# A two-layer graph network on one core: a tile in every 64 fetched by SyncE, 30 edge groups stored as cell matrices in pass 1, blocks normalized two at a time, and a second pass by a table of counts

## The chip, the cores and the metric

The program runs on one core of a Trainium2 chip. Its time is the device time of one execution in microseconds (us). The kernel before took 1641.12 us (median of 3 runs, 1638.93 to 1643.31).

## The reference

6250 nodes with 96 features and 100000 edges, sorted by destination. Exact GELU, no approximations:

```python
# layer 0, over edges (src -> dst)
e = concat(x[src], edge_attr)                     # 100000 x 128
msg  = gelu(e @ mW1 + mb1) @ mW2 + mb2
gate = sigmoid(gelu(e @ gW1 + gb1) @ gW2 + gb2)
agg  = segment_sum(msg * gate, dst)
h    = x + gelu(concat(x, agg) @ uW1 + ub1) @ uW2 + ub2
x    = layernorm(x + layernorm(h) * ln_g + ln_b)
# layer 1, GCN
deg  = segment_sum(edge_weight, dst) + 1;  dinv = rsqrt(deg)
g    = segment_sum((x @ W)[src] * dinv[src] * w * dinv[dst], dst) + self loop
x    = layernorm(x + g + b)
```

## The kernel before

The edges are cut into 98 groups of 8 tiles of 128 edges; the nodes into 49 blocks of 128. Each pass treats the groups in order.

**Pass 1.** For each group GpSimd gathers the 8 tiles of source rows from HBM by 8 indirect DMAs (`gathers`, L430) into one of 8 slots of `rows`; a slot comes free when TensorE has transposed the group that lay in it. In `step1` TensorE turns the rows (L520, into the PSUM pair `ps_xt`), multiplies them by both first-layer weights in two halves (L543, L546, into the pair `ps_hid`), and sums messages into a window of nodes by a matrix of ones and zeros (`window1`, L493, `ps_win`). ScalarE copies the turned rows (L769), takes the GELU (L784) and the gate's tanh (L803, `squash`); VectorE makes the 0/1 matrix (L1034), reduces the gate's logit (L1123, L1126), applies the gate (`gate1`, L1099 to L1102) and adds the window to `acc1` (L1051). Every second group one block of nodes is finished: `agg`, `upd_in`, `upd_out` on TensorE (L593 to L611), `upd_gelu` on ScalarE (L814), `block1a` on VectorE, which normalizes twice with an inverse root by Newton steps (`rsqrt`, L1081 to L1090).

**Cell matrices.** For some groups of pass 2 the sum over sources isn't gathered but computed as a product of all node features with a matrix of "cells" (source node by destination column). 24 of these matrices are made in pass 1, two tiles per step from group 2 on: `pair_hot` on VectorE (L1133, L1137), `pair_cells` on TensorE (L571, one tile through `ps_xt` at the step's start, one through `ps_hid` at its end), `pair_copy` on ScalarE (L824) into one of two buffers, and a store of both tiles by SyncE (L406) to `b_table`. The copy waits until the store before last of its buffer has landed.

**Pass 2** is a list of 40 turns, each with one dense group and the gathered groups listed before it (58 in all). Kind P loads its matrix from `b_table` (SyncE, L393) and multiplies (L645). Kind B (16 of them) is built in its own turn: `dense2` on VectorE, 8 tiles of `cells2` (L625) through the same PSUM pairs, then 49 products (L642). Gathered groups take 8 indirect DMAs and 8 products (L730) with weighted 0/1 matrices from VectorE (L1034, L1043). `turn_over` and `place_sums` (L715, L721) put the dense sums into the window; VectorE adds them (L1281). When a block's sources are complete, 3 blocks at a time are finished (`block2`, L692 and L1294 to L1309) and written out.

Each engine runs its own list in program order, tied to the others by semaphores. The order in a step of pass 1 is written out by hand; that of pass 2 comes from `second_pass()`:

```python
n = 0 if q in NONE_YET else (2 if KIND[q] == "B" else 1) + (q in ONE_MORE)
turns.append(GATHERED[taken:taken + n] + [d])
```

Of the kernel before, what the change touches and what calls it, by code (L numbers as in the profile page):

```python
# [5 lines left out]
P = 128  # L6
N, E = 6250, 100000
ND, ED = 96, 32
TG = 8
# [21 lines left out]
ROW = 12  # L31
STARTS = (0, 3, 5, 8, 10)
KINDS = "PBPBP"
FIRST_BUILT = KINDS.index("B")
NONE_YET = (0, 1)
ONE_MORE = (12, 22, 32)
MIXED = NG // ROW * ROW
DENSE = [g for g in range(MIXED) if g % ROW in STARTS]
KIND = [KINDS[d % len(KINDS)] for d in range(len(DENSE))]
# [3 lines left out]
GATHERED = [g for g in range(NG) if g not in DENSE]  # L43
DT = NTURN * TG
PAIRS = len(STORED) * TG // 2
PAIR_AT = 2
CELLS = 2 * HW
TURN_AFTER, PLACE_AFTER, SUMS_AFTER = 5, 11, 32
# [5 lines left out]
def second_pass():  # L54

    turns, taken = [], 0
    for q, d in enumerate(DENSE):
        n = 0 if q in NONE_YET else (2 if KIND[q] == "B" else 1) + (q in ONE_MORE)
        turns.append(GATHERED[taken:taken + n] + [d])
        taken += n  # L60
    turns.append(GATHERED[taken:])
    order = [g for turn in turns for g in turn]
    place = {g: n for n, g in enumerate(order)}
    added = {g: q for q, turn in enumerate(turns) for g in turn}
    parts = []
# [8 lines left out]
assert PAIR_AT + PAIRS == NG  # L74
# [3 lines left out]
def gnn_kernel(nc, t, out):  # L78
# [6 lines left out]
    x1s_table = nc.dram_tensor("x1s_table", [NP, ND], fp32, kind="Internal").ap()  # L85
    b_table = nc.dram_tensor("b_table", [len(STORED) * P, TG * CELLS], fp32, kind="Internal").ap()

    ctx = ExitStack()
    with ctx:
# [39 lines left out]
        crossed = sb("crossed", [NG, NW])  # L129
# [16 lines left out]
        idx = sb("idx", [P, NT], i32)  # L146
        rows = [sb(f"rows{v}", [P, TG, ND]) for v in range(SLOTS)]
# [1213 lines left out]
```

## Time and profile before

| | |
|---|---|
| profiled execution / its span | 1641.43 us / 1639.6 us |
| TensorE busy | 1435.3 us, 88% |
| GpSimd busy | 1178.4 us, 72% (1244 indirect DMAs) |
| VectorE busy | 1143.4 us, 70% |
| ScalarE busy | 559.8 us, 34% |
| granted TensorE clock, mean | 0.96 |
| DMA, mean | 126 GB/s |

Pass 1 fills the span up to about 1005 us, pass 2 the rest. Busy time counts executed work; the 0.30 us between two gathers on GpSimd, in which it issues, is not counted as busy. A record in the trace can end after the next begins, since matmuls are pipelined, so lengths are best read from start to start.

### The profile page before, as it was taken

To read this page: it belongs to the slowest core of one execution; us is meant where nothing else is said; L and a number is where in the kernel's file an instruction comes from. 1 tells how busy PE (TensorE), PEld (TensorE's weight loads), DVE (VectorE), ACT (ScalarE), POOL (GpSimd) and SP (SyncE) were. 2 spreads that over 40 slices of the span, in tenths; PEclk is the share of its full clock that TensorE was granted. 3 is DMA by queue.
4 is the path that set the end of the run, shared out by engine and by line. 5 is a ranking of instruction groups with operands and counts; after the bars stand their busy time and mean duration, and the time that the engine had idled before them with its cause. 6 is when DMAs were issued, how large, how long until landed. Compare 5 with 4: busy or idle time off the path is not lost.

```text
span 1639.6 us, 31556 instructions
## 1 busy us (share of the span) xinstructions
PE 1435.3 (88%) x11180; PEld 1273.6 (78%) x11181; DVE 1143.4 (70%) x3201; ACT 559.8 (34%) x985; POOL 1178.4 (72%) x1257
## 2 busy tenths in 40 slices
PE   3526999999999999999999987899999999998996
PEld 2415878787878778787877776799998989887986
DVE  5314889888988888889888887444654556555543
ACT  1103545454544545454544443111111111212110
POOL 7777777777777777777777770677777777777771
PEclk8767999999999999999999999999999999999997
DMA  3423444344444444444444443454544435353530
GB/s 106 123 67 109 133 120 131 115 134 116 134 117 126 124 127 125 115 134 118 133 116 127 122 116 115 130 173 125 168 143 126 165 104 167 101 191 102 196 112 19
DMA packets 80039, 205.95 MB, mean 126 GB/s; under 512 B 39325, under 2 KB 40893, under 8 KB 76703
## 3 DMA queue, kind: packets, MB, share of 16 engines
q1 hardware_dynamic: 28688, 127.68, 20.5%
q0 software_dynamic: 39808, 61.22, 17.4%
q10 hardware_dynamic: 11376, 14.90, 3.1%
q8 instruction: 95, 1.56, 0.4%
q14 instruction: 72, 0.59, 0.1%
HBM read 139.91 MB, written 63.80 MB: 124 GB/s over the span
## 4 chain that ended last, share of the span: by engine, by line
DVE 37%; PE 34%; DVEq 14%; issue 7%; DMA 3%; another core or an unknown queue 2%; POOL 2%; ACT 1%; ACTq 0%; POOLq 0%
DVE shared L1137 8%; PE ps_bt L642 8%; PE ps_win L730 5%; PE ps_xt L645 5%; PE ps_hid L645 4%; DVE logit L1126 4%; DVE shared L1133 3%; DVE edges L1102 3%; DVEq L1125 3%; PE ps_hid L625 3%; PE ps_xt L625 3%; DVEq L1049 2%; DVE prod L1123 2%; DVEq L1100 2%
## 5 line engine op out<-in xcount | busy, mean ns | idle before, releaser
L430 POOL DMA_INDIRECT rows<-in_x_nat,idx x782 | 740.5, 947 | 243.0 <-issue 237.0
L430 POOL DMA_INDIRECT rows<-x1s_table,idx x462 | 436.0, 944 | 184.6 <-issue 139.9
L546 PE MATMUL ps_hid<-w,edges 128*128 128x192 f32 x1568 | 325.2, 331 | 0.0
L546 PEld LDWEIGHTS ps_hid<-w,edges 128*128 128x128 f32 x1568 | 272.2, 194 | 14.3 <-issue 1.3
L1137 DVE TENSOR_TENSOR shared<-cell,ps_fix 128x1200 f32<-128x1200 f32 (+1 forms) x128 | 218.3, 1706 | 0.0
L784 ACT ACTIVATE edges<-ps_hid 128x768 f32<-128x768 f32 x196 | 159.1, 812 | 172.1 <-PE ps_hid L546 171.1
L1281 DVE TENSOR_TENSOR acc<-acc,ps_win 96x80 f32 x98 | 22.9, 234 | 240.2 <-PE ps_win L721 217.0
L493 PE MATMUL ps_win<-hot,edges 128*98 128x80 f32 x1568 | 156.1, 254 | 28.7 <-DVE acc L1051 28.6
L493 PEld LDWEIGHTS ps_win<-hot,edges 128*98 128x98 f32 x1568 | 148.8, 170 | 40.8 <-DVE edges L1102 39.1
L520 PE MATMUL ps_xt<-ident,rows 128*96 128x128 f32 x784 | 108.9, 284 | 71.9 <-ACT shared L824 40.2
L520 PEld LDWEIGHTS ps_xt<-ident,rows 128*96 128x96 f32 x784 | 89.2, 131 | 87.1 <-ACT shared L824 50.4
L543 PE MATMUL ps_hid<-b_split,ones_b 128*128 128x384 bf16 x392 | 129.9, 331 | 7.6 <-DVE step L998 5.9
L824 ACT ACTIVATE shared<-ps_hid 128x600 f32<-128x600 f32 x96 | 64.4, 671 | 189.6 <-PE ps_hid L571 189.6
L1034 DVE TENSOR_TENSOR hot<-dst_rel,ps_fix 128x640 f32<-128x640 f32 x156 | 126.6, 811 | 0.1
L769 ACT ACTIVATE edges<-ps_xt 96x1024 f32<-96x1024 f32 x98 | 100.0, 1020 | 72.3 <-PE ps_xt L520 68.6
L571 PE MATMUL ps_xt<-shared 128*128 128x300 f32 x384 | 114.4, 421 | 4.3 <-DVE shared L1137 4.3
L571 PE MATMUL ps_hid<-shared 128*128 128x300 f32 x384 | 116.2, 425 | 0.9 <-ACT edges L784 0.9
L730 PE MATMUL ps_win<-hot,rows 128*96 128x80 f32 x928 | 95.5, 264 | 21.6 <-DVE hot L1043 19.9
L1133 DVE TENSOR_SCALAR shared<-ps_fix,src_low,weight 128x128 f32<-128x128 f32 x320 | 112.6, 401 | 1.9 <-issue 1.9
L730 PEld LDWEIGHTS ps_win<-hot,rows 128*96 128x96 f32 x928 | 92.2, 180 | 26.4 <-issue 24.9
L824 ACT ACTIVATE shared<-ps_xt 128x600 f32<-128x600 f32 x96 | 64.4, 671 | 118.1 <-DVE edges L1102 53.4
L1126 DVE TENSOR_REDUCE logit<-prod 128x8 f32<-128x768 f32 x98 | 93.4, 953 | 7.2
(157 smaller groups left out, 2241.8 us busy)
## 6 DMA issues: line engine op xcount, KB each, us to landing
b_table<-shared SPq DMA_DIRECT2D x96, 600.0 KB, 3.4
edges<-b_table SPq DMA_DIRECT2D x12, 2400.0 KB
wide<-b_table SPq DMA_DIRECT2D x12, 2400.0 KB
rows<-in_x_nat,idx POOLq DMA_INDIRECT x782, 2.7
edges<-in_edge_t ACTq DMA_DIRECT2D x96, 128.0 KB
rows<-x1s_table,idx POOLq DMA_INDIRECT x462
wide<-in_x_t SPq DMA_DIRECT2D x1, 2376.5 KB
out_nodes<-y SPq DMA_DIRECT2D x49, 48.0 KB
```

The lines of the kernel that those rows point to most:

```text
L430: nc.gpsimd.indirect_dma_start(out=rows[slot][:, k, :], out_offset=None, in_=table, in_offset=bass.IndirectOffsetOnAxis(ap=idx[:, TG * g + ...
L493: mm = nc.tensor.matmul(ps_win[0:rws, 0:W], lhs[:, k, :], hot[u][:, k, :], start=(k == 0), stop=(k == TG - 1))
L520: mm = nc.tensor.transpose(ps_xt[m // 4][0:ND, P * (m % 4):P * (m % 4 + 1)], rows[v][:, m, :], ident[:, :])
L546: mm = nc.tensor.matmul(ps_hid[j][:, HC * q:HC * (q + 1)], feat[u][:, P * m:P * (m + 1)], w1[:, :], start=False, stop=(q == 1))
L571: mm = nc.tensor.matmul(ps_pair[i][:, m, 0:HW], pair_low[n % 2][:, i, :], pair_place[n % 2][:, 2 * i + m, :], start=True, stop=True)
L642: mm = nc.tensor.matmul(ps_bt[0:TW, 0:ND], unit_b[d % 2][:, TW * c:TW * (c + 1)], x_nat[:, c, :], start=(c == 0), stop=(c == NB - 1))
L645: mm = nc.tensor.matmul(raw_sums(d), x_nat[:, c, :], unit_b[d % 2].rearrange("p (k x) -> p k x", k=TG)[:, :, WD * c:WD * (c + 1)], start=( ...
L730: mm = nc.tensor.matmul(ps_win[0:ND, W * col:W * (col + 1)], rows[i % SLOTS][:, k, :], hot[i % 2][:, k, :], start=(k == 0), stop=(k == TG ...
L784: nc.scalar.activation(flat(hid[u][:, 4 * half:4 * half + 4, :]).rearrange("p (j c) -> p j c", j=2), ps_pair[1][:, :, 0:2 * HC], ACT.Gelu) ...
L1126: nc.vector.tensor_reduce(logit[u][:, :], prod[:, :, :], AX, ALU.add).then_inc(s_logit, 1)
L1133: nc.vector.tensor_scalar(low[:, i, :], places_ps[:, 0:P], src_low[:, TG * d + k:TG * d + k + 1], weight[:, TG * g + k:TG * g + k + 1], AL ...
L1137: return nc.vector.tensor_tensor(place, cells.to_broadcast(shape), places_ps.rearrange("p (o w) -> p o w", o=1).to_broadcast(shape), ALU.i ...
```

## The change

- **SyncE fetches rows.** In each of groups 15, 23, ..., 95 (11 groups) the last tile is no longer gathered by GpSimd. SyncE loads eight node numbers at a time into registers and issues one DMA per row, 128 per tile, 16 rows after the stores of each step.
- **30 groups stored, 11 built.** The rows of dense sites change (14 groups a row, 6 sites each, one left out). Pass 1 makes 240 tiles of cells, 2 and 3 in turn per step, in a ring of 5 places; each tile has its own store, into three buffers. In a step of three tiles the middle one takes `ps_xt` between the two halves, and the next group's rows are turned after the second half.
- **Blocks normalized in pairs.** VectorE does the first half of the work of two blocks in one step and the inverse root and the rest in the step two later.
- **Early groups.** Groups 1, 4, 6 and 7 are gathered for pass 2 before pass 1 ends, from a table of the first 41 blocks; sources in the last 8 blocks point to a row of zeros and are added by a small cell matrix (`early_part`).
- **Pass 2** has 41 turns, with the gathered groups (57) dealt out by the table `TAKES`; there is no turn after the last dense one. Stored matrices are loaded in halves.

```diff
-ROW = 12
-STARTS = (0, 3, 5, 8, 10)
-KINDS = "PBPBP"
+ROW = 14
+STARTS = (0, 3, 5, 8, 10, 12)
+MAKE = 11
+EARLY = (1, 4, 6, 7)
+DONE_B = 41
+MADE = (2, 3)
+READY = 3
+TAKES = (0, 0, 2, 2, 1, 2, 2, 1, 2, 2, 0, 1, 2, 2, 1, 2, 0, 0, 2, 1, 2, 1, 2, 2, 2, 1, 2, 2, 1, 2, 0, 2, 0, 1, 2, 1, 1, 2, 2, 2, 2)
+FAR = [SLOTS * k + FAR_V for k in range(1, ROUNDS)]
+FAR_ROWS, FAR_LOAD = P // SLOTS, 8
...
+            def far_rows(i, first, n, buf):
+                for r in range(first, first + n, FAR_LOAD):
+                    _, nodes = nc.values_load_multi_w_load_instructions(
+                        far_idx[i:i + 1, r:r + FAR_LOAD], engines=(mybir.EngineType.SP,), min_val=0, max_val=N - 1,
...
+                    for m, node in enumerate(nodes):
+                        sp.dma_start(far[buf][r + m:r + m + 1, :], t["x_nat"][ds(node, 1), :]).then_inc(s_far[buf], 16)
...
             def end1():
-                for n in range(PAIRS):
-                    p, v = n // (TG // 2), n % (TG // 2)
-                    sp.wait_ge(s_pair_out, 2 * n + 2)
-                    sp.dma_start(b_table[P * p:P * (p + 1), 2 * CELLS * v:2 * CELLS * (v + 1)], ready_b[n % 2]).then_inc(s_stored[n % 2], 16)
+                for n in range(BATCHES):
+                    for i in range(FIRST[n], FIRST[n + 1]):
+                        p, k = i // TG, i % TG
+                        sp.wait_ge(s_tile_out, i + 1)
+                        sp.dma_start(b_table[P * p:P * (p + 1), :].rearrange("p (h k x) -> p h k x", h=2, k=TG)[:, :, k, :],
+                                     ready_b[i % READY].rearrange("p (h x) -> p h x", h=2)).then_inc(s_stored[i % READY], 16)
+                    b = n // 2 - LAG - 5
+                    if n % 2 == 0 and 0 <= b < DONE_B:
+                        sp.wait_ge(s_xs, b + 1)
+                        sp.dma_start(x1s_early[P * b:P * (b + 1), :], x_nat[:, b, :]).then_inc(s_early, 16)
+                    if n < SLOTS * len(FAR):
+                        i = n // SLOTS
+                        if n % SLOTS == 0 and i >= 2:
+                            sp.wait_ge(s_xt, FAR[i - 2] + 1)
+                        far_rows(i, FAR_ROWS * (n % SLOTS), FAR_ROWS, i % 2)
...
# step1, TensorE
                     mm.then_inc(s_pre, 1)
-                    late = isinstance(g, int) and g >= NG - 2
+                    if more and half == 0:
+                        pe.wait_ge(s_tile_out, FIRST[n] + 1)
+                        tile_cells(FIRST[n] + 1, 0, n, g)
+                    late = more or isinstance(g, int) and g >= NG - 2
                     if half == late and not (isinstance(g, int) and g == NG - 1):
                         if building:
-                            pe.wait_ge(s_pair_out, 2 * (g - PAIR_AT) + 1)
-                        transposes(k + (v + 1) // SLOTS, (v + 1) % SLOTS)
+                            pe.wait_ge(s_tile_out, FIRST[n + 1] - 1)
+                        transposes(k + (v + 1) // SLOTS, (v + 1) % SLOTS, easy)
...
# ScalarE
+            def tile_copy(i, pair):
+                act.wait_ge(s_tile_cells, i + 1)
+                wait(act, s_stored[i % READY], 16 * (i // READY))
+                nc.scalar.activation(ready_b[i % READY].rearrange("p (m x) -> p m x", m=2),
+                                     ps_pair[pair][:, :, 0:HW], ACT.Copy).then_inc(s_tile_out, 1)
...
# VectorE
+            def pair1(b):
+
+                if b == 0:
+                    block1([0], [])
+                elif b % 2 == 0:
+                    block1_sums([b - 1, b], [0] if b == 2 else [b - 3, b - 2], True)
+                elif b > 1:
+                    block1_rows([b - 2, b - 1], [0] if b == 3 else [b - 4, b - 3], True)
...
# GpSimd
-            pool.wait_ge(s_xt, NG)
             with pool.If(hard < 1):
+                pool.wait_ge(s_zeroed, 16)
+                pool.wait_ge(s_early, 16 * DONE_B)
+                for i in range(NE):
+                    pool.wait_ge(s_xt, NG - SLOTS + i + 1)
+                    early_gathers(i)
+                pool.wait_ge(s_xt, NG)
                 pool.wait_ge(s_xsw, 16 * NB)
...
# pass 2, TensorE
                         dense_sums(q, range(0, NB))
+                        if q in EARLY_IN:
+                            early_part(q, EARLY_IN[q])
```

On TensorE, in the middle of pass 1, an odd group from its first tile of cells on stood so before (L571 cells, L543 and L546 the first layer, L520 transposes, L593 and L598 the block's sums):

```order
L571 MATMUL ps_xt<-shared 128x300 x2
L543 MATMUL ps_hid<-b_split,ones_b 128x384
L546 MATMUL ps_hid<-w,edges 128x192 x2
L543 MATMUL ps_hid<-b_split,ones_b 128x384
L546 MATMUL ps_hid<-w,edges 128x192 x2
L520 MATMUL ps_xt<-ident,rows 96x128 x8
L593 MATMUL ps_bt<-acc,mw 96x128
L543 MATMUL ps_hid<-b_split,ones_b 128x384
L546 MATMUL ps_hid<-w,edges 128x192 x2
L543 MATMUL ps_hid<-b_split,ones_b 128x384
L546 MATMUL ps_hid<-w,edges 128x192 x2
L598 MATMUL ps_bt<-wide,uw1x 96x128
```

and so in the changed kernel (L675 cells, L645 and L648 the first layer, L620 transposes, L692 the block's sums):

```order
L675 MATMUL ps_xt<-shared 128x300 x2
L645 MATMUL ps_hid<-b_split,ones_b 128x384
L648 MATMUL ps_hid<-w,edges 128x192 x2
L645 MATMUL ps_hid<-b_split,ones_b 128x384
L648 MATMUL ps_hid<-w,edges 128x192 x2
L675 MATMUL ps_xt<-shared 128x300 x2
L692 MATMUL ps_bt<-acc,mw 96x128
L645 MATMUL ps_hid<-b_split,ones_b 128x384
L648 MATMUL ps_hid<-w,edges 128x192 x2
L645 MATMUL ps_hid<-b_split,ones_b 128x384
L648 MATMUL ps_hid<-w,edges 128x192 x2
L620 MATMUL ps_xt<-ident,rows 96x128 x8
```

A third tile of cells has come between the halves, and the transposes have moved behind the second half. Even groups keep their order.

On VectorE, the block's work in an even group before (L1169 to L1195 statistics and centred rows, L1081 and L1083 the start of the inverse root):

```order
L1169 BN_STATS stats<-h 128x6
L1176 TENSOR_TENSOR h<-x_nat,ps_bn 128x96
L1178 TENSOR_SCALAR deg<-ps_bn 128x1
L1179 TENSOR_SCALAR rin<-ps_bn 128x1
L1182 TENSOR_TENSOR x1b<-x_nat,ln_b 128x96
L1186 BN_STATS stats<-h 128x6
L1189 BN_AGGR mv<-stats 128x2 x2
L1191 TENSOR_SCALAR rin<-mv 128x2
L1193 SCALAR_TENSOR_TENSOR h_g<-h,mv,ln_g 128x96
L1195 TENSOR_SCALAR h_c<-h,mv 128x96
L1081 TENSOR_SCALAR step<-rin 128x3
L1083 TENSOR_SCALAR root<-step 128x3
```

and in the changed kernel, in every second even group (the others hold the inverse root and what follows it):

```order
L1376 BN_STATS stats<-h 128x6 x2
L1384 TENSOR_TENSOR h<-x_nat,ps_bn 128x192
L1386 TENSOR_SCALAR deg<-ps_bn 128x2
L1387 TENSOR_SCALAR rin<-ps_bn 128x2
L1390 TENSOR_TENSOR x1b<-x_nat,ln_b 128x192
L1394 BN_STATS stats<-h 128x6 x2
L1397 BN_AGGR mv<-stats 128x2 x4
L1399 TENSOR_SCALAR rin<-mv 128x4
L1401 SCALAR_TENSOR_TENSOR h_g<-h,mv,ln_g 128x96 x2
L1403 TENSOR_SCALAR h_c<-h,mv 128x96 x2
L1294 TENSOR_TENSOR prod<-edges,ps_fix 128x768
L1297 TENSOR_REDUCE logit<-prod 128x8
```

Two blocks stand in one run of instructions, and the gate's product follows at once.

On SyncE, pass 1 before was its stores alone, with the first loads of pass 2 behind them:

```order
L406 DMA b_table<-shared 128x1200 x96
L393 DMA edges<-b_table 128x4800
L413 DMA x1s_table<-x_nat 128x96 x2
L393 DMA edges<-b_table 128x4800 x2
L393 DMA wide<-b_table 128x4800
```

Now the last row of one step, the three stores of the next and the first row after them read so (L456 loads eight numbers, the ISA row is register arithmetic, L460 fetches one row):

```order
L460 ISA
L460 DMA shared<-in_x_nat 1x96
L467 DMA b_table<-shared 256x1x300 x3
L456 TENSOR_LOAD shared
L460 ISA
L460 DMA shared<-in_x_nat 1x96
```

Between the stores of two steps there are 16 such rows and 2 loads, in 88 of the 96 steps that make cells.

## Rows read from the trace of the kernel before

**Rows 1.** The page, its first line.

```profile
span 1639.6 us, 31556 instructions
```

**Rows 2.** Windows of pass 2: busy us (x instructions) of each engine, clock, DMA.

```profile
1240.00:1600.00 360.00, 342.29 (x3230) 313.58 (x3229) 195.50 (x489) 66.18 (x126) 272.23 (x289) 0.98 0.44 141
```

**Rows 3.** The gathers on GpSimd (min/median/max ns, first and last start) and one wait.

```profile
L430 POOL DMA_INDIRECT rows<-in_x_nat,idx x782: 940/944/1698, 2.9 to 985.0; - x196
L430 POOL DMA_INDIRECT rows<-x1s_table,idx x462: 938/944/954, 1030.0 to 1605.6; - x154
...
  DMA x1s_table<-x_nat: 44.1, 1
```

**Rows 4.** Timeline of TensorE, two groups of pass 1: start us, length us, what.

```profile
501.31 1.17 PE L571 MATMUL ps_xt<-shared 128*128 128x300 f32 x4
...
509.05 1.58 PE L493 MATMUL ps_win<-hot,edges 128*98 128x80 f32 x16 [0.66 <-DVE acc L1051]
...
515.25 0.33 PE L543 MATMUL ps_hid<-b_split,ones_b 128*128 128x384 bf16 x1
...
516.88 0.38 PE L598 MATMUL ps_bt<-wide,uw1x 97*96 97x128 f32 x2
...
518.42 0.46 PE L611 MATMUL ps_bn<-uw,upd_t 97*128 97x96 f32 x2 [0.64 <-ACT upd_t L814]
518.72 1.20 PE L571 MATMUL ps_hid<-shared 128*128 128x300 f32 x4
519.76 1.17 PE L571 MATMUL ps_xt<-shared 128*128 128x300 f32 x4
```

**Rows 5.** Timeline of ScalarE in the same groups.

```profile
515.23 1.02 ACT L769 ACTIVATE edges<-ps_xt 96x1024 f32<-96x1024 f32 x1
...
517.08 0.81 ACT L784 ACTIVATE edges<-ps_hid 128x768 f32<-128x768 f32 x1 [0.33 <-PE ps_hid L546]
```

**Rows 6.** The chain of waits in the same groups: start us, length us, what.

```profile
505.35 0.63 DVE shared L1133 x2
505.98 1.31 DVE shared L1137
...
509.79 0.26 DVE stats L1169
...
511.65 0.18 DVEq L1080
...
514.83 0.33 DVE x_nat L1203
...
515.69 0.86 DVE prod L1123
```

**Rows 7.** Timeline of ScalarE near the start of pass 1.

```profile
135.96 0.67 ACT L824 ACTIVATE shared<-ps_xt 128x600 f32<-128x600 f32 x1 [39.10 <-DMA b_table<-shared]
```

**Rows 8.** SyncE's queue: two one- to three-row DMAs, and the landing of L406.

```profile
3.71 0.27 SPq L380 DMA_DIRECT2D shared<-in_mb  x1
4.02 0.28 SPq L380 DMA_DIRECT2D shared<-in_gb  x1
...
DMA to landing us min/median/max: 3.2/3.4/54.5
```

**Rows 9.** Groups by line, pass 2: busy us, mean ns, idle before.

```profile
L730 PE MATMUL ps_win<-hot,rows 128*96 128x80 f32 x928 | 95.5, 264 | 21.6 <-DVE hot L1043 19.9 <-issue 1.5
L625 PE MATMUL ps_hid<-shared 128*128 128x300 f32 x248 | 75.3, 427 | 0.0
...
L642 PE MATMUL ps_bt<-x_nat,edges 128*96 128x96 f32 x784 | 68.4, 249 | 0.0
```

**Rows 10.** Timeline: last transposes, first sums of pass 2, last dense sums copied.

```profile
991.95 1.04 PE L520 MATMUL ps_xt<-ident,rows 128*96 128x128 f32 x8
...
1020.62 9.46 PE L645 MATMUL ps_xt<-edges,x_nat 128*96 128x96 f32 x90
...
1616.91 0.25 ACT L909 ACTIVATE sum_cols<-ps_hid 96x96 f32<-96x96 f32 x1 [6.74 <-PE ps_hid L645]
```

More of the change, by code:

```diff
@@ L64, in second_pass @@
     added = {g: q for q, turn in enumerate(turns) for g in turn}
+    whole = dict(place)
+    for q, es in EARLY_IN.items():
+        for g in [EARLY[e] for e in es]:
+            added[g], whole[g] = max(added[g], q), max(whole[g], place[turns[q][0]])
     parts = []
@@ L422, in _, with early_gathers @@
             with sp.If(hard < 1):
                 end1()
+            with sp.Else():
+                for i in range(len(FAR)):
+                    sp.wait_ge(s_xt, FAR[i] - SLOTS + 1)
+                    far_rows(i, 0, P, 0)
         @block.gpsimd
         def _(pool):
-            def gathers(g, slot, table, rows_sem):
+            def early_gathers(i):
+                for k in range(TG):
+                    nc.gpsimd.indirect_dma_start(
+                        out=rows[slot_of(i)][:, k, :], out_offset=None, in_=x1s_early,
+                        in_offset=bass.IndirectOffsetOnAxis(ap=idx_early[:, TG * i + k:TG * i + k + 1], axis=0)).then_inc(
+                            s_rows2[i % SLOTS], 16)
@@ L428, in gathers @@
+            def gathers(g, slot, table, rows_sem, n):
                 last = g == NG - 1
-                for k in range(TG - (REST if last else 0)):
+                elsewhere = table is not x1s_table and g in FAR
+                for k in range(TG - (REST if last else 1 if elsewhere else 0)):
                     nc.gpsimd.indirect_dma_start(
@@ L676, in block1b @@
                 nc.tensor.transpose(ps_bt[0:ND, 2 * P:3 * P], x_nat[:, b, :] if easy else xs[:, :], ident[:, :]).then_inc(s_xst, 1)
-            run_pass(pe, step1, block1a, lambda b: block1b(b, False), ahead=True, even=LAG + 3, odd=LAG, end=end1, close=close1)
             def step2(k, v, easy, b):
@@ L857, in block1b @@
                 nc.scalar.activation(acc1[0:ND, ds(P * b, P)], ps_bt[0:ND, 2 * P:3 * P], ACT.Copy).then_inc(s_xstc, 1)
-            run_pass(act, step1, block1a, lambda b: block1b(b, False), ahead=True, even=LAG + 3, odd=LAG, end=end1, close=close1)
             def step2(k, v, easy, b):
@@ L938, in _ @@
             nc.vector.drain()
+            for g in EARLY:
+                nc.vector.memset(chosen[:, g:g + 1], 1.0)
             for r in STARTS:
```

503 lines of the change are left out of this document (333 added, 170 removed).

## Prediction, made before the run

> **What bounds the kernel now.** I began with the page's first line [rows 1]: the span is 1639.6 us of the profiled execution's 1641.43 us, so 1.8 us lie around it, and that execution is 0.3 us above the median of 1641.12. All sums below start from 1641.43.
>
> GpSimd's gathers show two stages [rows 3]: 782 from 2.9 to 985.0, one per 1.257 us, and 462 from 1030.0 to 1605.6, one per 1.249 us, with 44.1 us between in which it waits for the normalized table. That looks like an engine that sets the pace. The chain of waits says otherwise for pass 1: it runs on VectorE alone, from the cells' 0/1 matrix to the block to the gate's product [rows 6]. TensorE's timeline gives the period, 501.31 to 519.76, so 18.45 us for two groups, 9.23 each [rows 4], against the 8 x 1.25 = 10.0 that GpSimd needs. Both end together because TensorE starts late: near the start ScalarE stands 39.10 us, until 135.96, for the first store of cells [rows 7], and from there catches GpSimd up only at the end. The last transposes are at 991.95 [rows 10].
>
> Pass 2 runs from the first sums at 1020.62 to the last dense sums copied at 1616.91, then 22.7 us of tail to the span's end [rows 10, 1]. In it TensorE is nearly full: 342.3 of 360 us in the middle stretch, at a clock of 0.98 [rows 2]. GpSimd has little slack there, but TensorE is what lags.
>
> **Pass 1, VectorE.** One block costs 515.69 - 509.79 = 5.90 us, of which 514.83 - 511.65 = 3.18 is the inverse root [rows 6]. For two blocks the root is paid once, and most small instructions too. I cost the first half at 3.2 us (2.0 plus six added records of about 0.2) and the second at 3.2 + 0.9 + 0.7 = 4.8, so 8.0 for four groups in place of 11.8: 1.9 saved per two groups. The fifth tile per two groups adds half of 0.63 + 1.31 [rows 6], 0.97. VectorE goes from 18.45 to about 17.5 per two groups, and 18.3 in the pair with the root. It stops being the bound.
>
> **Pass 1, TensorE.** This then sets the pace, and its waits have to be followed. Of the 18.45 us, 0.66 is VectorE's window add [rows 4], and I take 0.5 of it away, plus 0.3 of a transpose that waits for a copy. The wait of 0.64 for the block's GELU stays [rows 4]. So the old loop without VectorE takes 17.6. The new tile costs 519.76 - 518.72 = 1.04 [rows 4]. The moved transposes add nothing of their own, but they are moved past the second GELU, and now ScalarE's row copy of 1.02 [rows 5] stands between that GELU and the block's. Before, the block's sums started at 516.88 and its last product at 518.42, 1.54 later [rows 4]; now it is 0.2 + 0.81 + 1.0 + 0.2 + 0.3 = 2.5 (GELU, row copy, tanh, block's GELU [rows 5]). That is 0.96 more, while the transposes' own 0.9 is taken out of the front of the step: 0.1 net. Sum 17.6 + 1.04 + 0.1 = 18.7 per two groups, 9.35 a group. The bounds are 17.7 (all waits gone) and 19.6 (18.45 + 1.04 + 0.1, no wait gone). I take 18.65, since VectorE has 0.3 us to spare even in the heavier pair.
>
> **Where pass 1 starts and ends.** The first stores still land at about 136. Before, the fifth cell tile needed them; with three one-tile buffers it is the fourth, so TensorE resumes with group 4's transposes instead of group 5's. That is one group later, about 9 us. Group 4 is turned at 136.7, group 96 at 136.7 + 46 x 18.65 = 994.6, group 97 one half step later, 9.8 us, at 1004.4. Before: 991.95. Pass 1 grows by 12.5 us, although GpSimd has 11 gathers (13.8 us) less to do. GpSimd's part is off the path: from 136 on it is held by the slots and needs 7 x 10.0 + 8.75 per eight groups, 9.84 each, against 9.33.
>
> **SyncE's rows.** Between the stores of two steps SyncE issues 16 one-row DMAs and 2 register loads. Small DMAs are issued 4.02 - 3.71 = 0.31 apart [rows 8], so 5.0 us is the lower end; if each register instruction cost as much as a DMA, 16 x 0.62 = 9.9. I take F = 6.5. Nobody waits for the rows (fetched a round ahead), but a store stands behind them. The first tile of an odd step is stored F after the last of the even step (10.1 + 0.35 into the pair), lands 3.4 later [rows 8], and the copy that needs its buffer comes at 1.15 in the next pair with 0.8 to spare: F may be 18.65 + 1.95 - 13.85 = 6.75. Beyond it the pair lasts (30.55 + F) / 2. So at 6.5 it costs nothing, barely. No row shows a register load on this queue. The Trainium skill, "DMA: Bandwidth & Descriptors", section "Latency and other measured facts", puts a floor of about 600 ns under such a load; by that F would be 5.0 + 1.2 = 6.2 with free arithmetic. The skill's "Runtime: NRT & Kernel Launch", section "Instruction fetch mechanics", has about 200 ns per register even in bulk, so 3.2 us for 16, F above 8.2. No run here shows which. That second rule gives the slower rival below.
>
> **Pass 2.** Work on TensorE: five built groups fewer, 40 tiles of cells at 1.04 from start to start (busy 1.21, 75.3 / 62 [rows 9]) = -41.6. One dense group more: 68.4 / 8 = 8.55 busy, 8.4 without the overlap [rows 9] = +8.4. One gathered group less: 95.5 / 58 = 1.65 with its slow ones, 1.4 = -1.4. The early part: 32 products of a third of a cell tile's half and 32 of the sums' chunks, near 0.17 each, with placing = +13. One more turn and six more turned over = +1.5. Together -20. The stored matrices' loads, in halves, have over a turn (12 us and more) to land; I cost them at nothing, and at up to 10 us if they collide.
>
> Waits: in the stretch of rows 2 TensorE is idle for 17.7 us, and the groups by line put 19.9 us of its idle time on VectorE's weighted matrix [rows 9], which comes late when a finished block or a built group is in VectorE's list. Five built groups fewer and the counts of the table should take about 10 us of idle time and slow clock. The tail of 22.7 had two gathered groups after the last dense sums, behind a late matrix; now they come with the sums: -6.5. Between the passes, step 97 has a third tile and one more block: +1.5. Sum -35, bounds -20 (the work alone) and -45. GpSimd doesn't stop this: the four early groups fill the gap of 44.1 us [rows 3], their 40 us ending some 8 us after the old start of the gathers, and 422 more take 527, against 577 before, so they end near 1004 + 46 + 527 = 1577, well before TensorE.
>
> Sum: 1641.4 + 12.5 - 35.5 = 1618.4. I forecast 1618.
>
> **Rivals.**
> 1. *SyncE paces pass 1 (slower).* With F = 9.0, near the upper end of 9.9, its own list, two times F and 2.2 for five stores, an early store and their waits, fills 20.2 us per two groups, 1.55 more; over 44 pairs +68: 1686. With F = 8.2 it is (30.55 + 8.2) / 2 = 19.4, +0.75, +33: 1651. It decides from the point where 44 x excess = 23, 19.17 per pair, F = 7.8. For it: the row price is for DMAs with constant addresses, and 1408 of them are added with register addresses. Against: 6.5 leaves 1.3 us per step. [...]
> 2. *TensorE's waits go, and GpSimd ends pass 1.* 771 gathers at 1.257 from 2.9, plus 14 us in which group 12 waits for group 4's slot at 136.7, end near 986; the last transposes 7 us later at 993. -11.5: 1607. If the waits of pass 2 go as well, 1597. For it: the old loop's waits were mostly VectorE's. Against: the GELU's wait can't go.
> 3. *Pass 2 gives little back.* Nine turns more go through HBM, at 2.4 MB each, and the gathers share the DMA engines. With the bound of -20 and 6 us of landing waits: 1641.4 + 12.5 - 14 = 1640, no change.
> 4. *The change doesn't do what it says*: a source outside the allowed window would send the program down its general path. The same inputs took the short path before; 1 in 100, and then far over any range.
>
> **How the numbers follow.** Forecast 0.48 (own range 1605 to 1632); rival 1 0.19; rival 2 0.20; rival 3 0.12; the last 0.01. A measurement tells about 0.3%, 5 us, from no change. Faster: 0.47 + 0.20 + 0.05 = 0.72. Within 0.3%: 0.01 + 0.03 of rival 1 + 0.05 of rival 3 = 0.09. Slower: 0.16 + 0.02 + 0.01 = 0.19. The range of 8 in 10 goes from 1596 (rival 2) to 1655 (the mild half of rival 1).
>
> **What would show it.** Pass 1 in TensorE's timeline: two groups in 18.6 to 18.8 us, the block's last product still waiting for ScalarE about 0.8, the window add waiting under 0.3. Group 4's transposes near 137, group 97's near 1004. SyncE's queue: 16 rows in under 6.75 us, and no wait of ScalarE's tile copy for a store after 140; such waits of 1 us and more in each pair would be rival 1. GpSimd waiting for slots from 125 on; if TensorE waits for rows of `in_x_nat` late in pass 1 instead, it is rival 2. The gap before pass 2's gathers filled by 32 gathers. From the last transposes to the span's end 612 us instead of 647.7; above 630 rival 3 holds. A pair above 19.2 us makes the forecast wrong.

## The result and the profile after

The changed kernel takes 1808.37 us, median of 4 runs (1804.12 to 1816.43), against 1642.01 of the kernel before beside it: ratio 1.1022, 95% interval 1.0979 to 1.1065. Forecast were 1618 us and a gain. The profiled execution took 1809.87 us, its span is 1808.1 [rows 1].

Four stretches split the difference of the two traces, which is 168.5 us of span [rows 1, 10]:

| part | before | after | forecast | came out |
| --- | --- | --- | --- | --- |
| start to the last transposes | 991.95 | 1176.97 | +12.5 | +185.0 |
| last transposes to first sums of pass 2 | 28.67 | 29.44 | +1.5 | +0.8 |
| first sums to last dense sums copied | 596.29 | 584.04 | -30 | -12.3 |
| from there to the span's end | 22.7 | 17.65 | -6.5 | -5.0 |

The places, from the timeline of TensorE and ScalarE (start us, length us, what), which answer to [rows 10]:

```profile
1176.97 1.04 PE L620 MATMUL ps_xt<-ident,rows 128*96 128x128 f32 x8
...
1206.41 8.91 PE L748 MATMUL ps_xt<-edges,x_nat 128*96 128x96 f32 x90
...
1790.45 0.25 ACT L1051 ACTIVATE sum_cols<-ps_hid 96x96 f32<-96x96 f32 x1 [6.20 <-PE ps_hid L748]
```

The chain of waits names the new pace-maker. SyncE's queue (SPq) does not appear in it in the kernel before, where VectorE led with 37%. By engine, shares of the span:

```profile
PE 48%; SPq 26%; issue 7%; DMA 7%; DVE 6%; ACT 4%; DVEq 2%; ACTq 0%
```

SyncE's queue over two groups of pass 1 (start us, length us, what; a row joins neighbours of one kind). L460 are the one-row DMAs, L467 the stores, L472 the early store. The gap ahead of each L460 row is the first of the step's two register loads; the second lies within its 16 DMAs:

```profile
705.49 1.88 SPq L467 DMA_DIRECT2D b_table<-shared  x3
708.94 7.64 SPq L460 DMA_DIRECT2D shared<-in_x_nat  x16
716.63 1.88 SPq L467 DMA_DIRECT2D b_table<-shared  x2
718.55 0.61 SPq L472 DMA_DIRECT2D x1s_early<-x_nat  x1
720.42 7.34 SPq L460 DMA_DIRECT2D shared<-in_x_nat  x16
727.81 1.87 SPq L467 DMA_DIRECT2D b_table<-shared  x3
```

From the end of the stores, 707.37, to the next one, 716.63, the rows hold the queue for F = 9.26 us in the odd step, and from 719.16 to 727.81 for 8.65 in the even one. The pair lasts 727.81 - 705.49 = 22.3 us; over the middle of pass 1 the mean is 22.6, and from 320 to 900 us F is 9.5 in odd and 9.0 in even steps on the mean. ScalarE's tile copies in the same pair, which answer to [rows 5, 7], show who feels it:

```profile
708.28 0.67 ACT L969 ACTIVATE shared<-ps_xt 128x600 f32<-128x600 f32 x1 [3.19 <-DMA b_table<-shared]
...
717.30 0.67 ACT L969 ACTIVATE shared<-ps_hid 128x600 f32<-128x600 f32 x1 [1.61 <-PE ps_hid L675]
```

One copy per pair waits about 3 us for a store to land, which SyncE issued only at 705.49, because the rows stood in front of it. TensorE stands 1.99 us behind that copy, and the window products after the wait take 2.49 us where 16 of them took 1.53 later in the pair. The granted clock from 710.03 to 712.5 is 0.57, so mostly the lower of its two levels; over 300 to 1100 it is 0.95 on the mean:

```profile
709.00 0.97 PE L620 MATMUL ps_xt<-ident,rows 128*96 128x128 f32 x7 [1.99 <-ACT shared L969]
...
710.03 2.49 PE L587 MATMUL ps_win<-hot,edges 128*98 128x80 f32 x16
714.68 1.53 PE L587 MATMUL ps_win<-hot,edges 128*98 128x80 f32 x16
...
725.22 0.46 PE L710 MATMUL ps_bn<-uw,upd_t 97*128 97x96 f32 x2 [0.85 <-ACT upd_t L960]
```

The same loop without rows can be seen in the same trace: SyncE has fetched its last row at 1124, and after that two groups take 1148.53 - 1129.80 = 18.73 us, the forecast's 18.65:

```profile
1129.80 1.04 PE L620 MATMUL ps_xt<-ident,rows 128*96 128x128 f32 x8
...
1148.53 1.04 PE L620 MATMUL ps_xt<-ident,rows 128*96 128x128 f32 x8
```

### The profile page after: what moved, and what is told of

It is laid out like the page before. It is cut to its first block, busy times and chain, and to the rows that moved or that the text cites. A ratio compares the mean times of both kernels' runs of the same rounds, so it can differ in the third digit from the quotient of the medians.

```text
span 1808.1 us, 36225 instructions
## 1 busy us (share of the span) xinstructions
PE 1496.4 (83%) x11438; PEld 1337.9 (74%) x11439; DVE 1112.7 (62%) x2921; ACT 567.2 (31%) x1007; POOL 1160.8 (64%) x1238
## 4 chain that ended last, share of the span: by engine, by line
PE 48%; SPq 26%; issue 7%; DMA 7%; DVE 6%; ACT 4%; DVEq 2%; ACTq 0%
SPq L460 11%; PE ps_win L587 9%; DMA b_table<-shared 7%; PE ps_hid L748 6%; PE ps_xt L748 5%; PE ps_bt L745 5%; SPq L440 5%; SPq L456 5%; PE ps_hid L648 4%; PE ps_win L834 4%; PE ps_xt L620 4%; ACT shared L969 3%; PE ps_hid L675 3%; PE ps_xt L675 2%; DVE shared L1308 2%
## 5 line engine op out<-in xcount | busy, mean ns | idle before, releaser
L517 POOL DMA_INDIRECT rows<-in_x_nat,idx x771 | 729.8, 947 | 371.7 <-issue 217.2
L517 POOL DMA_INDIRECT rows<-x1s_table,idx x422 | 398.2, 944 | 128.6 <-issue 127.1
L648 PE MATMUL ps_hid<-w,edges 128*128 128x192 f32 x1568 | 327.7, 333 | 0.0
L648 PEld LDWEIGHTS ps_hid<-w,edges 128*128 128x128 f32 x1568 | 276.2, 196 | 14.5 <-issue 1.4
L620 PE MATMUL ps_xt<-ident,rows 128*96 128x128 f32 x773 | 116.5, 300 | 192.8 <-ACT shared L969 171.2
L620 PEld LDWEIGHTS ps_xt<-ident,rows 128*96 128x96 f32 x773 | 93.3, 137 | 210.5 <-ACT shared L969 184.6
L1308 DVE TENSOR_TENSOR shared<-cell,ps_fix 128x1200 f32<-128x1200 f32 (+3 forms) x136 | 224.5, 1650 | 0.0
L1270 DVE TENSOR_SCALAR ps_fix<-squash 128x8 f32<-128x8 f32 x98 | 16.6, 170 | 309.1 <-ACT squash L949 306.3
L587 PEld LDWEIGHTS ps_win<-hot,edges 128*98 128x98 f32 x1568 | 174.6, 193 | 8.7 <-issue 6.6
L587 PE MATMUL ps_win<-hot,edges 128*98 128x80 f32 x1568 | 178.1, 275 | 2.8 <-DVE acc L1222 1.9
L969 ACT ACTIVATE shared<-ps_xt 128x600 f32<-128x600 f32 x144 | 96.5, 670 | 264.9 <-DMA b_table<-shared 232.9
L675 PE MATMUL ps_xt<-shared 128*128 128x300 f32 x576 | 170.3, 419 | 4.3 <-DVE shared L1308 4.3
L645 PE MATMUL ps_hid<-b_split,ones_b 128*128 128x384 bf16 x392 | 132.1, 337 | 5.9 <-DVE step L1163 4.9
L675 PEld LDWEIGHTS ps_xt<-shared 128*128 128x128 f32 x576 | 108.8, 191 | 34.9 <-DVE shared L1308 4.6
L675 PE MATMUL ps_hid<-shared 128*128 128x300 f32 x384 | 117.1, 428 | 0.0
L834 PE MATMUL ps_win<-hot,rows 128*96 128x80 f32 x912 | 92.0, 260 | 22.1 <-DVE hot L1214 16.3
```

Source lines behind the costliest of these rows:

```text
L517: nc.gpsimd.indirect_dma_start(out=rows[slot][:, k, :], out_offset=None, in_=table, in_offset=bass.IndirectOffsetOnAxis(ap=idx[:, TG * g + ...
L587: mm = nc.tensor.matmul(ps_win[0:rws, 0:W], lhs[:, k, :], hot[u][:, k, :], start=(k == 0), stop=(k == TG - 1))
L620: mm = nc.tensor.transpose(ps_xt[m // 4][0:ND, P * (m % 4):P * (m % 4 + 1)], tile, ident[:, :])
L645: nc.tensor.matmul(ps_hid[j][:, 0:2 * HC], ones_b[:, :], flat(b1_split[:, :, :]), start=True, stop=False)
L648: mm = nc.tensor.matmul(ps_hid[j][:, HC * q:HC * (q + 1)], feat[u][:, P * m:P * (m + 1)], w1[:, :], start=False, stop=(q == 1))
L675: mm = nc.tensor.matmul(ps_pair[pair][:, m, 0:HW], ring_low[:, i % RING, :], ring_place[:, 2 * (i % RING) + m, :], start=True, stop=True)
```

## The experiments

Theory 1 after this reading: SyncE's queue paces pass 1. Rivals: TensorE's longer loop at a lowered clock; stores that land late because of the buffers or the crowded DMA engines.

### Without the rows, with fixed rows, with one DMA, with half of them

no_rows, the row fetch undone and all else kept:

```diff
-FAR = [SLOTS * k + FAR_V for k in range(1, ROUNDS)]
+FAR = []
```

> SyncE fetches no rows; GpSimd gathers all eight tiles of every group again; everything else is as in the changed kernel. Theory 1 (SyncE's own list paces pass 1: per two groups two sets of 16 rows at 9.26 us, five stores and the rest 3.8, 22.3 in all): the pair falls to 18.7 us, as it is after batch 88, where no rows are left; ScalarE's tile copies wait for stores under 0.3 a pair; the last transposes near 1005 instead of 1177; total 1636 (1622 to 1648). Rival A (TensorE's longer loop under a lowered clock is itself near 21 us): the pair stays above 20.5, total above 1730. Rival B (three buffers and half-kilobyte pieces make the stores land late whatever else is in the queue): the copies still wait over 2 us a pair, total above 1720.

Measured: 1643.68 us, ratio to the kernel before 1.0015 (1.0001 to 1.0029). Pair 18.75 us, last transposes at 1006.72, no tile copy waiting for a store between 200 and 900, granted clock 1.00 from 300 to 900. The row fetch costs 165 us, all of the loss. That is theory 1's case; rivals A and B fall. The rest of the change, 1643.7 against 1640.9, gains nothing.

fixed_rows, the same DMAs from addresses known beforehand:

```diff
-                    for m, node in enumerate(nodes):
-                        sp.dma_start(far[buf][r + m:r + m + 1, :], t["x_nat"][ds(node, 1), :])...
+                    for m in range(FAR_LOAD):
+                        node = (1009 * (P * i + r + m)) % N
+                        sp.dma_start(far[buf][r + m:r + m + 1, :], t["x_nat"][node:node + 1, :])...
```

> The same 1408 one-row DMAs into the same places, but from addresses known beforehand and with no register loads (the rows are other nodes' rows, so that the tile's features are wrong). Theory 1: a row costs SyncE about 0.31 us instead of 0.41 and the loads are gone, F 5.0 instead of 9.26 us, list 13.8 a pair, under TensorE's 18.7: pair 18.7, total 1636 (1622 to 1650). Rival C (the 1408 small DMAs crowd the stores on the DMA engines): the traffic is the same, so pair near 22 and total near 1800.

Measured: 1642.27 us (one run), pair 18.75. The DMA engines carry the same 1408 rows and nothing is lost, so rival C falls. Its queue:

```profile
564.86 4.73 SPq L458 DMA_DIRECT2D shared<-in_x_nat  x16
569.64 3.91 SPq L465 DMA_DIRECT2D b_table<-shared  x3
573.60 5.00 SPq L458 DMA_DIRECT2D shared<-in_x_nat  x16
```

16 rows in 4.7 to 5.2 us, so 0.31 each, as [rows 8] had it. With a register address a row takes 0.41 us (16 in 6.5 to 6.9 us in load16 below): two register instructions of 37 and 29 ns with their gaps, and the DMA.

one_dma was to keep the register loads and replace the rows by one DMA:

```diff
+                sp.dma_start(far[buf][first:first + n, :], t["x_nat"][P * i + first:P * i + first + n, :])...
```

> The two register loads of a step stay, its 16 one-row DMAs are replaced by one DMA of 16 rows that lie together (other nodes' rows). Theory 1: F = 2 x 0.95 + 0.5 = 2.4 us, pair 18.7, total 1636 (1622 to 1650). If the register loads and not the rows were what stops the queue (they wait for everything before them, for instance), F would stay above 7 and the total above 1700.

Measured: 1647.99 us (one run), pair 18.75. Its trace holds no register load, so it shows only that one DMA of 16 rows per step (0.62 us, median) costs little or nothing; of the loads it tells nothing.

half_rows: SyncE fetches the tile of every sixteenth group.

```diff
-FAR = [SLOTS * k + FAR_V for k in range(1, ROUNDS)]
+FAR = [SLOTS * k + FAR_V for k in range(1, ROUNDS, 2)]
```

> SyncE fetches the tile of every sixteenth group only (6 groups, 768 rows in 48 steps), GpSimd gathers the other five. Theory 1: a step with rows costs what it costs now, one without nothing: 24 pairs at 22.3 and the rest at 18.7, so 1808 - 20 x 3.6 = 1736 (1720 to 1755). If the stores wait for crowded DMA engines, the loss falls more than in proportion, total under 1700.

Measured: 1728.93 us, ratio 1.0549 (1.0501 to 1.0598). As theory 1 has it: the cost goes with the number of steps that fetch. ScalarE's waits for stores fall from 168 us (55 times, between 200 and 1100 us) to 87 us (27 times).

### What a load costs, and how much room the queue had

load16, one load of 16 numbers per step:

```diff
-FAR_ROWS, FAR_LOAD = P // SLOTS, 8
+FAR_ROWS, FAR_LOAD = P // SLOTS, 16
```

> The changed kernel with one register load of 16 node numbers per step instead of two of 8. Of the 9.26 us that a step's rows hold SyncE, 16 x 0.41 = 6.6 are the rows, so 1.35 each the two loads. If a load costs the same whatever it brings, F falls to 7.9, SyncE's list to 19.6 per two groups, and the total by 44 x 2.7 = 119 to 1690 (1670 to 1710). If it costs per register, F stays 9.2 and the total 1808 (1795 to 1815).

Measured: 1785.27 us, ratio 1.0877 (1.0852 to 1.0902). Neither case of the expectation came: 23 us came back, not 119 and not 0. The load of 16 takes 2.145 us (median), that of 8 took 0.92, so its price grows with the registers, and my split, two fixed prices of 1.35, was wrong. F fell a little all the same, to 9.3 and 8.7 on the mean, and the pair from 22.6 to 22.0; which part of the two loads' time was saved is not shown. The changed kernel, then load16 (ns min/median/max):

```profile
L456 SPq TENSOR_LOAD <-shared x176: 683/920/2222, 133.0 to 1119.8; - x176
```

```profile
L456 SPq TENSOR_LOAD <-shared x88: 1295/2145/2644, 132.6 to 1089.4; - x88
```

fixed_24: rows with constant addresses, 24 per step, the eight more into an unused place.

```diff
                         far_rows(i, FAR_ROWS * (n % SLOTS), FAR_ROWS, i % 2)
+                        for m in range(8):
+                            ...
+                            sp.dma_start(far_more[r:r + 1, :], t["x_nat"][node:node + 1, :]).then_inc(s_far[i % 2], 16)
```

> As with constant addresses, but 24 rows per step instead of 16 (the eight more go to a place that nobody reads; the far tiles hold other nodes' rows). F = 24 x 0.31 = 7.5 us. If SyncE's whole list decides (2 F + 3.8 = 18.8 per two groups against TensorE's 18.7), nearly nothing is lost: 1642 to 1650. If the first store of an odd step is late as the prediction's second formula has it, (30.55 + 7.5) / 2 = 19.0, then 1642 + 44 x 0.3 = 1656. If the prediction's 0.31 does not hold for longer rows of such DMAs, more.

Measured: 1712.85 us, ratio 1.0436 (1.0404 to 1.0468), pair 20.3. F is 7.6 us, and it costs 70 us where the two formulas allowed up to 9 and 15. The granted clock from 300 to 900 is 1.00, so no slow clock enters here. Its queue, and ScalarE's copies beside it:

```profile
559.75 1.86 SPq L465 DMA_DIRECT2D b_table<-shared  x3
561.65 5.29 SPq L456 DMA_DIRECT2D shared<-in_x_nat  x16
566.99 2.32 SPq L478 DMA_DIRECT2D shared<-in_x_nat  x8
569.35 2.52 SPq L465 DMA_DIRECT2D b_table<-shared  x2
571.92 0.61 SPq L470 DMA_DIRECT2D x1s_early<-x_nat  x1
572.57 5.04 SPq L456 DMA_DIRECT2D shared<-in_x_nat  x16
577.65 2.47 SPq L478 DMA_DIRECT2D shared<-in_x_nat  x8
580.16 1.97 SPq L465 DMA_DIRECT2D b_table<-shared  x3
```

```profile
563.06 0.67 ACT L969 ACTIVATE shared<-ps_xt 128x600 f32<-128x600 f32 x1 [2.43 <-DMA b_table<-shared]
...
570.66 0.67 ACT L969 ACTIVATE shared<-ps_hid 128x600 f32<-128x600 f32 x1 [1.84 <-PE ps_hid L675]
```

Here the chain can be read off. The store at 559.75 has landed at 563.06, where the copy that needs its buffer starts (3.3). ScalarE and TensorE then need until 571.33 to finish the even step's last copy (8.3), its store and the early store end at 572.57 (1.2), and the odd step's first store, for which the next pair's copy waits, stands behind the rows until 580.16 (7.6). Sum 20.4. That is theory 2: one closed chain per pair, 12.8 + F, and the whole of F is in it. SyncE's whole list, 2 x 7.6 + 3.8 = 19.0 us, would fit into less than these 20.4. The threshold is then 18.75 - 12.8 = 6.0 us of rows.

rows_first tests it. The same 24 rows are issued ahead of the step's last store:

```diff
                     for i in range(FIRST[n], FIRST[n + 1]):
+                        if i == FIRST[n + 1] - 1:
+                            rows_of(n)
                         sp.wait_ge(s_tile_out, i + 1)
```

> 24 rows of constant addresses per step, as in the run of 1713 us, but issued ahead of the step's last store, not behind it: the same work on SyncE's queue. Theory 2 (one closed chain per pair: a store's landing, the tile copy that waits for it, half a step to the next copy, that tile's store and the rows behind it): the rows run while the step's last tile is still made, and what is left is TensorE's 18.75 or SyncE's list of 2 x 7.7 + 3.8 = 19.2: total 1713 - 44 x 1.1 = 1664 (1645 to 1675). If the sum of SyncE's work is what decides, nothing changes: 1713.

Measured: 1646.75 us, ratio 1.0032 (1.0015 to 1.0049), pair 18.8. The place in the queue alone is worth 66 us:

```profile
561.62 1.18 SPq L477 DMA_DIRECT2D b_table<-shared  x2
562.84 4.85 SPq L456 DMA_DIRECT2D shared<-in_x_nat  x16
567.74 2.28 SPq L468 DMA_DIRECT2D shared<-in_x_nat  x8
570.06 0.52 SPq L477 DMA_DIRECT2D b_table<-shared  x1
570.62 0.61 SPq L482 DMA_DIRECT2D x1s_early<-x_nat  x1
571.27 1.18 SPq L477 DMA_DIRECT2D b_table<-shared  x2
572.50 4.99 SPq L456 DMA_DIRECT2D shared<-in_x_nat  x16
```

The rows now run from 562.84 to 570.02, while ScalarE makes the step's last tile, and its store and the next step's follow at once. Sum and order are two different limits: 24 rows just fit into the queue's sum (it has no gap left, and the pair is 18.8), and did not fit into the chain. The 1664 expected came from a list of 19.2, a little too long. This does not rescue the changed kernel: with F of 8.7 to 9.3 the list alone, five stores of 0.63 and an early store included, is 21.7 us, above 18.75 in any order.

### The start, and what pass 1 could be

xt_split: no rows, and the load of the transposed node features, 97 partitions, as two.

```diff
-            sp.dma_start(x_t[:, :], t["x_t"]).then_inc(s_nodes, 16)
+            sp.dma_start(x_t[0:ND, :], t["x_t"][0:ND, :]).then_inc(s_nodes, 16)
+            sp.dma_start(x_t[ND:ND + 1, :], t["x_t"][ND:ND + 1, :]).then_inc(s_nodes, 16)
```

> No rows by SyncE, and the load of the transposed node features, 97 partitions in one DMA, is given as two: 96 partitions and 1. Theory on the start: the 97 partitions go over one DMA engine, and the first stores of cells, which queue behind it there, land only at 136 us; split, the fourth group is turned before 70 us instead of at 137. Then GpSimd sets the end of pass 1: 782 gathers at 1.257 us from 3 on, 986, and the last transposes 7 us later at 993 instead of 1006.7: total 1643 - 14 = 1629 (1622 to 1636). If the first stores wait for something else, no change: 1643.

Measured: 1624.94 us, ratio 0.9906 (0.9880 to 0.9931). It is 0.9% under the kernel before, clear of the interval. But the split is no part of the change, and the kernel before was not run with it except as below, on a chip whose times do not compare. The wait near the start [rows 7] is gone: group 4 is turned at 62.80, where it was 134.25 in no_rows. From there on GpSimd sets the pace, 20.0 us per pair; its last gather of pass 1 is at 983.63, the last transposes at 990.65.

```profile
62.80 1.04 PE L618 MATMUL ps_xt<-ident,rows 128*96 128x128 f32 x8
...
990.65 1.04 PE L618 MATMUL ps_xt<-ident,rows 128*96 128x128 f32 x8
```

SyncE's queue shows how the load held the stores, first in no_rows, then in xt_split:

```profile
40.54 88.06 SPq L438 DMA_DIRECT2D x1s_early<-y  x1
129.58 10.42 SPq L465 DMA_DIRECT2D b_table<-shared  x6
```

```profile
13.50 20.62 SPq L439 DMA_DIRECT2D x1s_early<-y  x1
49.74 89.84 SPq L466 DMA_DIRECT2D b_table<-shared  x24
```

In no_rows a DMA of 48 KB holds the queue for 88 us, and the first store of cells is not even issued before 129.58. The DMA records beneath say why: the features move in 97 pieces of 25088 bytes, one per partition. In no_rows they go one after another, about 1.05 us apart, from 23.3 to 128.9 us; in xt_split 16 and more are under way at once, and the last ends at 36.6. The kernel before has the same row of single pieces, from 23.5 to 129.9. That the single pieces all go over one DMA engine, as the expectation has it, fits this; the records do not name the engine.

xt_load16: the changed kernel's rows, one load of 16, with the split load of the features.

> The changed kernel with its rows, one load of 16 per step, and the transposed features loaded as 96 partitions and 1. TensorE starts some 75 us earlier, and SyncE's list of 19.6 us per two groups has that much more time: 60 + 44 x 19.6 + 2.5 x 18.7 = 969; GpSimd's 771 gathers end at 972, last transposes near 980, total 980 + 633 = 1613 (1605 to 1630). Should a load cost per register, F stays 9.26: 60 + 44 x 22.3 + 47 = 1088, total 1721.

Measured: 1719.35 us, ratio 1.0480 (1.0458 to 1.0502), last transposes 1077.96, pair 22.05. It is the second case of the expectation. The early start leaves the pair at 22, and the whole loop moves forward: the last transposes come 72 us before load16's 1149.87, and the total is 66 us lower. Without rows the same split gave 19, because there GpSimd takes over as the bound.

### Pass 2: the early part

no_early, on xt_split: the four early groups are gathered after pass 1 like the others, and the early part of the two built turns is gone.

```diff
-EARLY_IN = {BUILT[0]: (0, 1), BUILT[1]: (2, 3)}
+EARLY_IN = {}
```

> The kernel without SyncE's rows and with the split load of the features (1625 us), but the four early groups are gathered like all others after pass 1: no early gathers, and no early part in the two built turns. In the kernel with them the early parts hold TensorE 17 us and keep it waiting 5 more. Theory: TensorE has 22 us less to do, GpSimd 32 gathers more after pass 1 (454 x 1.25 = 567 us from about 1029, until 1597), so GpSimd nearly sets the end: 1597 + 20 = 1617 (1610 to 1627). If the early gathers are worth what the prediction credits them (TensorE waits for rows in the first turns), 1635 to 1650.

Measured: 1627.17 us, ratio 0.9914 (0.9887 to 0.9942), no difference from xt_split (0.9906) and 10 us above the 1617 expected. GpSimd stands idle between the passes again, and TensorE then waits for its rows, 19.5 us in seven places:

```profile
1027.87 0.94 POOL L516 DMA_INDIRECT rows<-x1s_table,idx  x1 [44.83 <-DMA x1s_table<-x_nat]
...
1593.46 0.94 POOL L516 DMA_INDIRECT rows<-x1s_table,idx  x1 [0.30 <-issue]
```

```profile
PE ps_win L827 <- DMA rows<-x1s_table,idx: 19.5, 7, 4.6
```

So the early gathers are worth about the 22 us that their own part costs TensorE, and no more.

### Runs that tell nothing

Eight more runs, in two groups, fell on a chip on which the kernel before took 2484 and 2522 us in place of 1641, with TensorE's granted clock at 0.79 to 0.83 and long waits without a releaser. Neither the changed kernel nor no_rows was run there, so even the ratios can't be split into the change and the experiment: 20 fixed rows per step 2605 and 2637 us, rows_first 2613 and 2652, no_early 2721 (these two are the ones given above from another chip), 8 rows per step with the split load 2609 and 2646, and the kernel before with the split load 2515, ratio 0.9974 (0.9956 to 0.9992). What was expected of those that weren't run elsewhere:

> Rows with constant addresses, 20 per step: F = 20 x 0.32 = 6.4 us (24 gave 7.7 and a period of 20.3 us, 16 gave about 5.1 and 18.75). Revised theory 2, one closed chain through every pair: a store lands 3.3 us after its issue, the tile copy that waits for it, 8.3 us of ScalarE and TensorE to the last copy of the even step, that tile's store and the early store 1.2, and then one step's rows: 12.7 + F = 19.1, 15 us over the 16 rows: total 1658 (1650 to 1666). By the prediction's formula (30.55 + 6.4) / 2 = 18.5, nothing is lost: 1642; by SyncE's whole list (2 F + 3.8 = 16.6) neither.

> The kernel before with nothing changed but the transposed features loaded as 96 partitions and 1. TensorE is released early there too, but its last transposes at 991.95 stand only 6 us behind the last of GpSimd's 782 gathers, which start at 3 and take 1.257 us each whatever TensorE does, save for the few us in which they wait for a slot. Theory: GpSimd ends pass 1 at 985 to 992 as before, and the total stays 1641 (1636 to 1643). If the 39 us of the start are on the path of the kernel before, it falls to 1615 or less.

> The transposed features as 96 partitions and 1, and SyncE fetches by node number 8 rows per step, one register load each, for five groups (23, 39, 55, 71, 87); GpSimd gathers the rest, 777. F = 8 x 0.41 + 1.4 = 4.7, chain 17.4 and list 13.2, both under the 20.0 us per pair at which GpSimd holds pass 1 here. Theory: pass 1 ends 5 x 1.257 = 6.3 us earlier than without the rows, total 1625 - 6 = 1619 (1614 to 1624). If rows cost time in themselves, 1625 or more.

So the threshold of 6.0 us rests on 5.1 being free, 7.6 costing 70 us and the chain read between them. Whether few enough rows on SyncE pay stays open, and so does what the split load gives the kernel before.

## Why the prediction was wrong

Taken by its own steps.

**SyncE's rows, the step that failed.** It said: 16 rows and 2 loads hold the queue 6.5 us, F may be 6.75, "So at 6.5 it costs nothing, barely". Both numbers were wrong. F came out at 8.7 to 9.3 in the pair shown, at the upper end of the bounds of 5.0 and 9.9: a row took 0.41 us and not 0.31, and a load of 8 took 0.92. I had two row prices and two bounds far apart, took the value that lay under a threshold I had just worked out, and named no row that it was nearest to. The threshold was wrong too. The sum behind the 6.75, a store issued F after 10.45, landing 3.4 later and needed 1.95 into the next pair, is already the closed chain: solved for the pair it gives 11.9 + F. In its place I wrote (30.55 + F) / 2, which counts only half of F and for which there was no row. The traces show 12.8 + F: all of F counts, once per pair, and the threshold at about 6.0 (inferred from the sum of fixed_24; 5.1 free and 7.6 costly are shown). At F = 6.5 itself the chain gives 19.3 a pair, +24 us; the forecast had no gain left even with its own F. What I had not followed is the place in the queue: the rows stand between the last store of one step and the first of the next, where the chain passes (rows_first).

**Rival 1** was the right mechanism at 0.19, with the right test ("such waits of 1 us and more in each pair would be rival 1"), and mis-sized: 20.2 us per pair at F = 9.0, where 22.6 came. It had SyncE's list, 2F + 2.2. The stores cost more than allowed: L467 takes 0.53 us against 0.32 before, and in a row they are 0.63 apart. With these the list is 2F + 3.8 = 21.7 for the two F seen, the queue nearly full. The chain of that pair is 22.3: 2.8 to the landing, 9.7 to the end of the even step's last copy, 1.2, and 8.65 of rows. Against fixed_24 the 9.7 is 1.4 more, which goes with TensorE's lower clock behind the wait. 44 pairs at 22.6 against 18.75 are the 170 us by which no_rows and the changed kernel part at the last transposes (1176.97 - 1006.72).

The prediction weighed two rules of the Trainium skill. By "Runtime: NRT & Kernel Launch", "Instruction fetch mechanics", two loads of 8 at about 200 ns per register would be 3.2 us, a price that page gives for loads from HBM, while these come from on-chip memory; by the floor of about 600 ns in "DMA: Bandwidth & Descriptors", "Latency and other measured facts", they would be 1.2. Measured were 2 x 0.92 = 1.8 us, between the two and nearer the floor. The floor held for the smallest load (683 ns) and said nothing of the growth; per register the loads of 8 and 16 took 0.12 and 0.13 us. That F passed the 8.2 of the first rule is owed to the rows, 6.6 us for 16 in place of 5.0.

**VectorE and TensorE in pass 1** came out as worked out. Pair 18.65 forecast, 18.73 to 18.75 measured; the block's last product waits 0.85 (0.8); the window add's wait is gone; group 4's transposes at 136.4 (136.7). In no_rows the last transposes are at 1006.7, forecast 1004.4. One sign did not come: GpSimd was to wait for slots from 125 on, and in no_rows it waited 10.6 us at 136 and from 200 to 980 only 2.1 us in all. Its last gather stands at 992.1, so TensorE still ended the pass, by 15 us.

**Pass 2.** -35 forecast, -16.5 in the changed kernel and -14.3 in no_rows. (Its four terms add up to -35.0; the forecast's sum took 35.5.) Three terms held: TensorE is busy 553.5 us in the dense stretch against 572.6, so -19.1 where the early and built work was set at -20; the tail -5.0 (-6.5); between the passes +0.8 (+1.5). The term that failed is "about 10 us of idle time and slow clock". Idle time in the stretch went from 23.7 to 30.6 us. TensorE still waits 16.3 us there for VectorE's weighted matrix; before, 15.4 of the 19.9 us in [rows 9] lay in this stretch and the rest in the tail:

```profile
L834 PE MATMUL ps_win<-hot,rows 128*96 128x80 f32 x912 | 92.0, 260 | 22.1 <-DVE hot L1214 16.3 <-issue 5.0
...
L844 PE MATMUL ps_hid<-shared 128*128 128x96 f32 x32 | 4.5, 283 | 3.3 <-DVE shared L1323 3.3
```

The same wait as a total, how often, and the longest, before and after:

```profile
PE ps_win L730 <- DVE hot L1043: 15.4, 8, 4.0
```

```profile
PE ps_win L834 <- DVE hot L1214: 16.3, 5, 4.1
```

Five built groups fewer did not mean less of it, and the cells of a built group (2.6) and the early part (3.3) add 6 of their own. I had let the wait shrink with the number of built groups. VectorE's timeline in no_rows shows what it hangs on: in a built turn that also finishes three blocks, the blocks' root and scaling (6 us, here 1380.87 to 1386.8) stand ahead of the sums' adds and the next weighted matrix, while TensorE's cells take 8 to 9:

```profile
1380.87 0.77 DVE L1521 SCALAR_TENSOR_TENSOR h<-ps_bn,dinv,x1b 128x96 f32<-128x96 f32 x3
...
1385.83 1.00 DVE L1536 TENSOR_SCALAR y<-h,mv,root 128x96 f32<-128x96 f32 x3
...
1390.25 0.82 DVE L1211 TENSOR_TENSOR hot<-hot,ps_fix 128x640 f32<-128x640 f32 x1
```

```profile
1391.17 5.38 PE L831 MATMUL ps_win<-hot,rows 128*96 128x80 f32 x32 [4.22 <-DVE hot L1211]
```

Such waits are fewer now, 5 in place of 8, and longer, 3.3 us on the mean in place of 1.9. That is read, not tested. Without the failed SyncE step the total would have been 1642 to 1644, near rival 3's 1640, "no change", which had 0.12. But that agreement is in the number alone. Rival 3 had the stored matrices landing late, in nine more turns (it is six, 30 stored matrices in place of 24), and the list of TensorE's waits in the changed kernel's dense stretch has no such load in it.

**GpSimd** did not end pass 1 (rival 2). It does so once the start's wait is gone, as xt_split shows, at 990.65 against the 993 worked out.

## What to carry to other kernels

Before giving a queue more work, follow one buffer around: from a store's issue to its landing, to the copy that waits for it, to the next store behind the new work. If that chain closes, the full length of the new work is in it, once per round, however empty the queue is on average; putting the work ahead of a store that is not yet ready can take it out of the chain. The queue's sum is a second limit, and both must hold. And when a bound of two prices spans a threshold, forecast from the dearer end, unless a row decides.

## What the runs showed of the hardware

A one-row DMA costs SyncE 0.31 us with a constant address and 0.41 with a register one, and the registers themselves 0.12 to 0.13 us each to load from on-chip memory, so a row fetched by its number cost the queue 0.54 to 0.58 us in the pair shown. Storing a tile as 256 pieces of 1200 bytes takes 0.53 us of the queue; 128 pieces of 4800 bytes took 0.32. One load of 97 partitions moved its 97 pieces one after another for 105 us and held up SyncE's next DMAs behind it, so that in no_rows the first store of cells was issued at 129.6 us and ScalarE waited 49 us for it. Given as 96 partitions and 1, with 16 and more pieces under way at once, it was done at 36.6 us, and that wait was gone.
